# Attention output with four column tiles on TensorE: sums of four key tiles on GpSimd, row maxima transposed before they are negated

## The reference

```python
Q = Q * cos + rotate_half(Q) * sin
K = K * cos + rotate_half(K) * sin
scores = jnp.einsum('bhqd,bhkd->bhqk', Q, K) / scale
scores = jnp.where(causal, scores, -jnp.inf)
attn = jax.nn.softmax(scores, axis=-1)
out = jnp.einsum('bhqk,bhkd->bhqd', attn, V)
return out.transpose(0, 2, 1, 3).reshape(B, S, H) @ Wo.T + bo
```

## Time and profile before

| | before |
|---|---|
| median of 3 runs (lowest to highest) | 755.08 us (752.31 to 756.74) |
| the profiled execution: its time | 756.7 us |
| its span in the profile | 754.9 us |
| TensorE busy, granted clock | 732.0 us, 0.995 of full speed |
| VectorE, ScalarE, GpSimd busy | 442.2, 308.7, 246.4 us |
| DMA | 104.39 MB, 138 GB/s mean |

### The profile page before, as it was taken

The page is one execution under the profiler, slowest core; times in us unless marked ns, Lnnn a source line. Parts: engine busy times, 40 slices in busy tenths (PEclk is TensorE's granted clock), DMA queues, the critical chain, the costliest instruction groups (busy, mean ns, idle before and its releaser), DMA issues.

```text
span 754.9 us, 10665 instructions
## 1 busy us (share of the span) xinstructions
PE 732.0 (97%) x3563; PEld 537.5 (71%) x3563; DVE 442.2 (59%) x1103; ACT 308.7 (41%) x641; POOL 246.4 (33%) x224
## 2 busy tenths in 40 slices
PE   7999999979999999999999999999999999999996
PEld 7788888755665655555555547878788888888884
DVE  6979584987777777777777637863243125114113
ACT  3232232256666666666655562223322232222221
POOL 0626251502114142414141436832232223223222
PEclk9999999999999999999999999999999999999998
DMA  8586568635566666666676475650001001001001
GB/s 281 187 280 232 197 251 278 251 127 158 167 168 180 166 177 181 170 180 175 167 194 167 111 208 171 250 227 1 0 3 55 0 1 56 0 0 56 1 1 58
DMA packets 54318, 104.39 MB, mean 138 GB/s; under 512 B 14820, under 2 KB 18404, under 8 KB 53748
## 3 DMA queue, kind: packets, MB, share of 16 engines
q1 hardware_dynamic: 54264, 103.72, 44.7%
HBM read 69.62 MB, written 38.21 MB: 143 GB/s over the span
## 4 chain that ended last, share of the span: by engine, by line
PE 83%; issue 5%; DVE 4%; DMA 3%; ACT 2%; POOL 2%; SPq 0%; DVEq 0%; POOLq 0%; ACTq 0%
PE ps L1101 38%; PE ps L1240 17%; PE ps L1316 9%; PE ps L1219 8%; PE ps L1126 8%; DMA q_st<-neg_max_T 2%; PE ps L1093 2%; POOL hid_lo L592 1%; ACT p L680 1%; ACT o_raw L687 1%; PE ps L1137 1%; PE ps L1160 1%; SPq L421 0%; DMA x_st<-in_x 0%; DVE stats L796 0%
## 5 line engine op out<-in xcount | busy, mean ns | idle before, releaser
L680 ACT ACTIVATE p<-ps 128x384 f32<-128x384 f32 (+3 forms) x384 | 159.5, 489 | 35.0 <-PE ps L1219 34.4
L841 DVE CUSTOM_DVE_ANT_0 masked<-ps,mask_qk 128x512 bf16<-128x512 f32 (+1 forms) x240 | 113.6, 502 | 66.9 <-PE ps L1126 66.0
L1219 PE MATMUL ps<-q_st,k_st 99*128 99x384 f32 (+2 forms) x384 | 135.6, 361 | 4.2 <-ACT p L680 1.3
L1240 PE MATMUL ps<-p,v_slot 128*64 128x512 f32 (+3 forms) x768 | 137.3, 494 | 0.2 <-ACT o_raw L687 0.2
L1052 DVE SCALAR_TENSOR_TENSOR hid<-ps,us_sb,silu 128x512 f32<-128x512 f32 x44 | 33.0, 751 | 165.2 <-PE ps L1101 159.5
L1126 PE MATMUL ps<-k_st,q_st 96*128 96x512 f32 (+2 forms) x384 | 127.8, 355 | 1.0 <-DVE row_max L841 0.9
L592 POOL TENSOR_TENSOR hid_lo<-hid,hid_hi 128x512 fp32r<-128x512 f32 x44 | 56.8, 1292 | 172.2 <-ACT hid_hi L756 172.2
L561 POOL TENSOR_SCALAR_AFFINE_SELECT p<-p 128x512 f32<-128x512 f32 x64 | 40.7, 637 | 202.9 <-ACT p L680 202.8
L1240 PEld LDWEIGHTS ps<-p,v_slot 128*64 128x64 f32 x768 | 50.1, 136 | 74.3 <-issue 62.0
L1126 PEld LDWEIGHTS ps<-k_st,q_st 96*128 96x128 f32 x384 | 72.5, 190 | 26.4 <-issue 17.7
L1219 PEld LDWEIGHTS ps<-q_st,k_st 99*128 99x128 f32 x384 | 72.3, 190 | 18.7 <-ACT p L680 9.6
(11 more groups left out here) (119 smaller groups left out, 1081.9 us busy)
## 6 DMA issues: line engine op xcount, KB each, us to landing
qk_scratch<-st_hi SPq DMA_DIRECT2D x32, 512.0 KB, 3.8
q_st<-qk_scratch SPq DMA_DIRECT2D x32, 384.0 KB, 3.9
k_st<-qk_scratch SPq DMA_DIRECT2D x32, 384.0 KB, 5.0
flag_st<-in_ffn SPq DMA_DIRECT2D x32, 264.0 KB, 2.8
ffn_copy<-in_ffn SPq DMA_DIRECT2D x32, 264.0 KB, 3.2
qk_scratch<-st_lo SPq DMA_DIRECT2D x16, 512.0 KB, 3.8
o_T<-o_raw SPq DMA_DIRECT2D x32, 128.0 KB, 4.6
rec_l<-rec_rows SPq DMA_DIRECT2D x32, 128.0 KB, 3.3
```

Source lines behind the costliest of these rows:

```text
L680: act.activation(p32[:, at:at + q0 + w - keep], ps[:, ST_BANK + i % ST_RING, keep - q0:w], ACT.Exp, scale=SCALE).then_inc(exp_done, 1)
L841: ins = dve.tensor_tensor_reduce((masked_a if u < 2 else masked)[:, s_before(i) % 2, col:col + kept], scores, mask_qk[:, 512 - kept:512], ...
L1219: pe.matmul(ps[:, ST_BANK + i % ST_RING, 0:w], k_st[0:K_ALL, slot, kt * P:(kt + 1) * P], q_st[0:K_ALL, slot, q0:q0 + w], start=True, stop= ...
L1240: ins = pe.matmul(ps[VW * a:VW * (a + 1), o_bank(u, half), q0 - 512 * half:512], v_slot[:, slot, kt, :], p32[:, at:at + n], start=(kt == 0 ...
```

## The change

P of key tiles 0 to 3 has no mask in the second half of the queries. The changed kernel sums these four tiles there, once for each head, on GpSimd (`sum_p`, three additions of 128x512), between the two masks, and takes l of those keys from one product with the sum. The products of the second half have 32 weight columns, and each head has two column tiles of its own: "v" rows (V of key tiles 0 to 3 or 0 to 5) and, in the other 32 rows, "l" (ones with P or with the sum) and "w" (V of the last two key tiles, in other PSUM columns). The second half is cut in two quarters of 256 queries, parts 1 and 2. "v" and "w" are two parts of the same result, so o_raw gets 512 more columns, SyncE two more moves for a pair (to o_w), and GpSimd one more addition for four heads. The inverses are loaded into the last group of o_T, and for the last group into a buffer in the place of P. The output weights are loaded at head 30 and not at the start. VectorE's test is done in two halves. The maxima are transposed at entry 3, ahead of the group, as they are; ScalarE writes the negated high word out of PSUM, VectorE the low one.

The core of the diff ("..." marks what is left out):

```diff
-M_ENTRY = 4
-M_AFTER = 3
+M_ENTRY = 3
+M_AFTER = 2
 S_BANKS = [[piece] for piece in S_PIECES[:-2]] + [S_PIECES[-2:]]
 S_BANKS.insert(M_ENTRY, [])
...
-PV_GROUPS = [[(0, 0), (0, 1), (0, 2), (0, 3)], [(1, 0), (1, 1)], [(1, 2), (1, 3), (1, 7)], [(1, 4), (1, 5), (1, 6)]]
+PV_GROUPS = [
+    (0, [[("vl", 0)], [("vl", 1)], [("vl", 2)], [("vl", 3)]]),
+    (1, [[("v", 0), ("w", 4)], [("v", 1), ("l", None)], [("v", 2), ("l", 4)], [("v", 3), ("l", 5)], [("w", 5)]]),
+    (2, [[("v", 0), ("w", 6)], [("v", 1), ("l", None)], [("v", 2), ("l", 4)]]),
+    (2, [[("v", 3), ("l", 5)], [("v", 4), ("l", 6)], [("v", 5), ("l", 7)], [("w", 7)]]),
+]
...
+PARTS = 3
+PART_DONE = (2, 4, 4)
+QW = 256
+SUM_KT = KT // 2
+SUM_SLOTS = 3
...
-            o_raw = sb("o_raw", [P, 2, S], F32, under_xT)
-            rec_l = sb("rec_l", [P, S], F32, under_xT)
+            o_raw = sb("o_raw", [P, 2, S + 2 * QW], F32, under_xT)
...
+                sp.wait_ge(o_evac, PARTS * (u + 1))
                 if u % 2 == 0 and u >= 2:
                     sp.wait_ge(l_out, 16 * (u // 2))
+                if u == PAIRS - 2:
...
                     t = 2 * u + a
                     rows = slice(t % 4 * D, (t % 4 + 1) * D)
-                    sp.dma_start(o_T[rows, t // 4, :], o_raw[2 * D * a:2 * D * a + D, u % 2, :]).then_inc(o_moved[u % 2], 16)
-                    sp.dma_start(l_cols[:, t % 4, :], o_raw[2 * D * a + D:2 * D * a + D + 1, u % 2, :].rearrange("o (p e) -> o p e", e=KT)).then_inc(o_moved[u % 2], 16)
+                    v_rows, l_rows = slice(VW * a, VW * a + D), slice(VW * a + D, VW * (a + 1))
+                    sp.dma_start(o_T[rows, t // 4, :], o_raw[v_rows, u % 2, 0:S]).then_inc(o_moved[u % 2], 16)
+                    sp.dma_start(l_cols[:, t % 4, :], o_raw[VW * a + D:VW * a + D + 1, u % 2, 0:S].rearrange("o (p e) -> o p e", e=KT)).then_inc(o_moved[u % 2], 16)
+                    sp.dma_start(o_w[t // 4 % 2][rows, :], o_raw[l_rows, u % 2, S:S + 2 * QW]).then_inc(o_moved[u % 2], 16)
 
             def store_rec(g):
...
                     load_head(t + SLOTS, t % SLOTS)
+                if t == HEADS - 2:
+                    sp.wait_ge(st_ps, NPC * t)
...
 
                 pool.wait_ge(rec_in, 64 * (g + 1))
-                pool.tensor_tensor(o_T[:, g, :], o_T[:, g, :], rec_l[:, :], ALU.mult).then_inc(o_scaled, 1)
+                pool.tensor_tensor(o_T[:, g, S // 2:S], o_T[:, g, S // 2:S], o_w[g % 2][:, :], ALU.add).then_inc(o_joined, 1)
+                pool.wait_ge(o_joined, g + 1)
+                pool.tensor_tensor(o_T[:, g, :], o_T[:, g, :], rec_of(g), ALU.mult).then_inc(o_scaled, 1)
                 pool.wait_ge(o_scaled, g + 1)
                 pool.tensor_scalar(o_T[:, g, :], o_T[:, g, :], bv_sb[:, g % KC:g % KC + 1], None, ALU.add).then_inc(o_done, 1)
...
+            def sum_p(t):
+
+                def second_half(kt):
+                    at = t % SLOTS * P_SIZE + P_OFF[kt] + S // 2 - P * kt
+                    return p32[:, at:at + S // 2]
+
+                total = p_sum[:, t % SUM_SLOTS, :]
+                if t >= SUM_SLOTS:
+                    pool.wait_ge(p_sum_read, 2 * ((t - SUM_SLOTS) // 2 + 1))
+                pool.tensor_tensor(total, second_half(0), second_half(1), ALU.add).then_inc(p_sum_step, 1)
+                pool.wait_ge(p_sum_step, 2 * t + 1)
+                pool.tensor_tensor(total, total, second_half(2), ALU.add).then_inc(p_sum_step, 1)
+                pool.wait_ge(p_sum_step, 2 * t + 2)
+                pool.tensor_tensor(total, total, second_half(3), ALU.add).then_inc(p_summed, 1)
+
...
             for t in range(HEADS):
                 copy_v(t)
                 if t % 4 == 0 and t >= 8:
                     scale_group((t - 8) // 4)
-                mask_p(t)
+                mask_low(t)
+                sum_p(t)
+                mask_high(t)
...
+                def max_high(u):
+                    act.wait_ge(max_T_ps, u + 1)
+                    act.activation(neg_hi_T[:, u % 2, :], ps[0:KT, M_BANK, 0:P], ACT.Copy, scale=-1.0).then_inc(max_hi, 1)
...
-            def evacuate_half(u, half):
...
+                act.wait_ge(pv_part[part], PART_DONE[part] * (u + 1))
...
+                    act.wait_ge(o_moved[u % 2], 96 * (u // 2))
+                src = ps[:, o_bank(u, part), :]
+                if part == 0:
+                    act.copy(o_raw[:, u % 2, 0:S // 2], src).then_inc(o_evac, 1)
+                else:
+                    dst = o_raw[:, u % 2, S // 2:S + 2 * QW].rearrange("p (s q c) -> p s q c", s=2, c=QW)
+                    act.copy(dst[:, :, part - 1, :], src.rearrange("p (s c) -> p s c", c=QW)).then_inc(o_evac, 1)
...
+            def whole_max(u):
+
+                dve.wait_ge(s_max, NS * (u + 1))
+                if u > 0:
+                    dve.wait_ge(max_T_ps, u)
+                dve.tensor_reduce(max8[:, :], row_max[:, u % 2, :, :], AX_X, ALU.max).then_inc(max_ready, 1)
+
+            def max_low(u):
+
+                dve.wait_ge(max_hi, u + 1)
+                dve.scalar_tensor_tensor(out=neg_lo_T[:, u % 2, :], in0=ps[0:KT, M_BANK, 0:P], scalar=-1.0,
+                                         in1=neg_hi_T[:, u % 2, :].bitcast(F32), op0=ALU.mult, op1=ALU.subtract).then_inc(max_T, 1)
...
+                for half in range(2):
+                    if t == 0 and half == 0:
+                        dve.wait_ge(flag_init, 1)
+                    else:
+                        dve.wait_ge(flag_done, 2 * t + half)
+                    cols = slice(half * FFN_PIECE // 2, (half + 1) * FFN_PIECE // 2)
+                    dve.scalar_tensor_tensor(out=flag_bits[:, :], in0=flag_st[:, cols].bitcast(I32), scalar=(1 << 12) - 1,
+                                             in1=flag_bits[:, :], op0=ALU.bitwise_and, op1=ALU.bitwise_or).then_inc(flag_done, 1)
...
             def transpose_max(v):
                 pe.wait_ge(max_ready, v + 1)
-                if v + 1 < HEADS:
-                    pe.wait_ge(s_max, NS * (v + 1) + s_before(M_ENTRY - S_RING) + 1)
                 if v > 0:
                     pe.wait_ge(max_T, v)
-                pe.transpose(ps[0:2 * KT, M_BANK, 0:P], neg_max[:, :].bitcast(F32), ident[:, :]).then_inc(max_T_ps, 1)
+                pe.transpose(ps[0:KT, M_BANK, 0:P], max8[:, :], ident[:, :]).then_inc(max_T_ps, 1)
...
+            def output_product(u, a, part, kind, kt):
+
+                slot, bank = (2 * u + a) % SLOTS, o_bank(u, part)
+                q_end = S // 2 if part == 0 else S // 2 + QW * part
+                q_low = 0 if part == 0 else q_end - QW
+                q0 = q_low if kt is None else max(P * kt, q_low)
+                if kt is None:
+                    probs = p_sum[:, (2 * u + a) % SUM_SLOTS, q0 - S // 2:q_end - S // 2]
+                else:
+                    at = slot * P_SIZE + P_OFF[kt] + q0 - P * kt
+                    probs = p32[:, at:at + q_end - q0]
+                row = VW * a
+                if kind == "vl":
+                    rows, weights, col = slice(row, row + VW), v_slot[:, slot, kt, :], q0 - q_low
+                elif kind == "v":
+                    rows, weights, col = slice(row, row + D), v_slot[:, slot, kt, 0:D], q0 - q_low
+                elif kind == "l":
+                    rows, weights, col = slice(row + D, row + VW), v_slot[:, slot, 0, D:VW], q0 - q_low
+                else:
+                    rows, weights, col = slice(row + D, row + VW), v_slot[:, slot, kt, 0:D], QW + q0 - q_low
+                ins = pe.matmul(ps[rows, bank, col:col + q_end - q0], weights, probs,
+                                start=((kind, part, kt) in PV_FIRST), stop=((kind, part, kt) in PV_LAST), skip_group_check=True)
+                if kt is None and part == 2:
+                    ins.then_inc(p_sum_read, 1)
+                if (kind, part, kt) in PV_LAST and kind != "l":
+                    ins.then_inc(pv_part[part], 1)
+
...
+                part, rounds = PV_GROUPS[group]
...
+                elif group == 1:
+                    pe.wait_ge(p_summed, 2 * u + 2)
                     pe.wait_ge(p_high_masked, 2 * u + 2)
...
+                for products in rounds:
                     for a in range(2):
...
+                        for kind, kt in products:
+                            output_product(u, a, part, kind, kt)
```

More of the change, by code:

```diff
@@ L273, in transformer_block @@
         p_high_masked = sem("p_high_masked")
-        pv_half = [sem(f"pv_half{k}") for k in range(2)]
+        p_sum_step = sem("p_sum_step")
+        p_summed = sem("p_summed")
+        p_sum_read = sem("p_sum_read")
+        pv_part = [sem(f"pv_part{k}") for k in range(PARTS)]
         o_evac = sem("o_evac")
@@ L338, in t_bank, with o_bank, rec_of @@
             return MM_BANK + j if n == N_CH else T_BANK + (j + 2) % TJ
-        def o_bank(u, half):
-            return ST_BANK if (u, half) == (PAIRS - 1, 1) else O_BANK
+        def o_bank(u, part):
+            return (O_BANK, ST_BANK + 2, ST_BANK)[part] if u == PAIRS - 1 else O_BANK
+        def rec_of(g):
```

(2 more changed lines are left out.)

133 lines of the change are left out of this document (56 added, 77 removed).

## The result

The changed kernel takes 761.99 us (median of 4 runs, 758.43 to 763.00), the one before 753.71 beside it. The ratio is 1.0081, 95% interval 1.0046 to 1.0116: **slower by 0.8%**, where a faster kernel, 749 us, was forecast. The profiled execution took 761.53 us, its span is 760.0. That of the kernel before (756.7 and 754.9) lies 3.0 us above its median, so the spans differ by 5.1 us where the medians differ by 8.3.

What follows compares the result with a forecast made beforehand. TensorE, busy 97% of the span, was taken as the bound. Terms -20.5 - 1.0 - 1.5 + 9 + 8.3 = -5.7 us took the span from 754.9 to 749.2; forecast 749 us, range 736 to 768.

Steps and rivals of the forecast that it cites:

- output products, four tiles at once: Stage B, second half: four column tiles overlap fully, 768 columns fewer, -1.28 us a pair, -20.5 us over 16 pairs.
- early transposes and what they free: Maxima transposed ahead of group 0: cost and freed exponential taken as 0; early transposes no longer waiting for the negation, -1.0 us.
- DMA stalls of the maxima: Maxima leave for q_st earlier in odd steps, so TensorE stands less for them: -1.5 us (bounds 0, -2.5).
- six post-scaling steps: VectorE's test meets GpSimd's sums after a scaling; score banks wait about 1.5 us, six times: +9 us (bounds 0, +11.4).
- to the last pair's start, in sum: Forecast terms for stage B up to the last pair's start, together -12.7 us.
- last pair and passage (-1.3 + 8.3): End of stage B into C1: last pair's shorter groups -1.3 us, late chunk 2 +8.3 us.
- I take 0 for the two, bounds -6 and +6: Stage B: transpose waiting 0.1 to 0.2 us a step, against some 0.4 us a pair from the exponential; net 0.
- The collisions: After scalings, test halves on VectorE each wait for the end of a GpSimd addition; TensorE's score banks wait 1.5 us.
- The passage: Stage B to C1: late sums, scalings and moves start chunk 2 5 to 9 us late, +8.3 us (bounds +5, +10).
- the rival of 805: Output products: only two run at a time, groups 1 to 3 3.0 us a pair longer, about 805 us; chance 0.16.
- Masks and copies: By the skill's port rule these GpSimd instructions also delay VectorE's test: 0.4 us in 14 steps, 5 us more, 754.
- GpSimd as the bound: Rival in stage B: additions at 1.75 us make GpSimd the bound and eat the gain, 758 to 768; chance 0.13.

Runs made afterwards that it cites:

- e6: Kernel before the change with 64 unused bytes laid between xT and everything above it: 761.69 us, ratio 1.0076 to before.
- e9: Changed kernel with 192 more unused bytes between xT and everything above it, a multiple of 256 bytes apart again: 755.00 us, ratio 0.9991 to before.
- e5: Changed kernel with 64 more unused bytes between xT and everything above it: 759.83 us, ratio 1.0057 to before.
- e1: Changed kernel with 96 unused bytes a partition laid under xT, moving all later tiles together: 760.88 us, ratio 1.0074 to before.
- e12: e9 with each of VectorE's test halves cut from 264 columns to 8, most weights untested: 747.56 us, ratio 0.9915 to before.
- e8: e5 with GpSimd's sums cut from 512 columns to 8 from the fourth head on: 758.20 us, ratio 1.0024 to before.
- e11: e9 with the maxima transposed after the first group again (M_ENTRY 4, M_AFTER 3, as before the change): 769.82 us, ratio 1.0186 to before.

## Why the prediction was wrong, step by step

| step of the prediction | forecast | measured |
|---|---|---|
| output products, four tiles at once | -1.28 a pair | -1.30 a pair |
| early transposes and what they free | 0, and -1.0 | third gap +0.37 a pair, others +0.04 to +0.13 |
| DMA stalls of the maxima | -1.5 | second gaps -2.0 |
| six post-scaling steps | +9 | +3.6 |
| to the last pair's start, in sum | -12.7 | -10.7 |
| last pair and passage (-1.3 + 8.3) | +7.0 | +10.9 |
| stage A, C2 | no term | +0.8, +4.1 |

Between the -5.7 us of the sum and the +5.1 of the two spans lie 10.8 us: 4.9 in stage A and C2, 3.9 in the last pair and the passage, 2.0 in the pairs before.

- **The step that failed is one that isn't there.** The sum has no term for C2 and stage A, since their instructions are the same. The run of tile sizes in the diff moved xT against the weights by a distance that isn't a multiple of 256 bytes; e6 and e9 show it both ways: 4.8 to 5.0 us in C2's matmuls; in the medians 6.7 us (e6 over the 755.02 beside it) and 4.8 to 5.9 (e5 and e1 over e9). With it repaired (e9) the change makes no difference that can be measured, 0.9991.
- **"I take 0 for the two, bounds -6 and +6"** was mis-sized. Both parts came as told: the transpose costs TensorE 0.16 us in most steps, and the exponential gave 0.3 us back. But that balances only the even steps. In the odd ones nothing was given back, and smaller delays came with the new order: the score bank behind a group takes 0.34 us to the next start, and the piece ahead of a group 0.40 where it took 0.33. +6 us was the upper bound; the lengthened gaps make +5.5 in the third and about +1.7 in the others over 15 pairs. The -1.0 for the early transposes belongs ahead of the first output products and was booked with the pairs; there those waits did go.
- **The collisions** are the right mechanism at 0.6 us, not 1.5: a test half lost half a microsecond, not a whole addition. That error went the other way.
- **The passage** went as told, in its cause, its place and its wait (4.9 us ahead of chunk 2, 0.6 ahead of chunk 1, 2.2 in the last pair, where 1.3 was said; 7.7 us together, 8.3 in the sum). What the forecast left out is the slower mask (0.9 of the 2.2 us) and the clock behind the waits, 4.2 us: -1.3 + 7.7 + 4.2 = 10.6 of the 10.9.
- **Output products**: the Trainium skill (TensorE: Matmul & The Clock Gate, Part 3, "The mechanism") has matmuls start and end in program order. The prediction drew from this that four tiles would be no faster than two, which doesn't follow: tiles that start together and end together keep that order. Groups 2 and 3 take 1.43 and 1.44 us, which only four overlapping tiles give, so the rival of 805 fell. The order of products isn't refuted by it; only the two records of one product don't both come ahead of the next product's first, as rows 4 showed before.
- **Masks and copies**: by the Trainium skill (SBUF — State Buffer, the rules on the shared port pair) they collide with the test as well. The copy's median is 589 ns in the changed kernel, 399 without the test (e12) and 397 without the sums (e8), so the rule holds for the copy; the masks stay at 0.64 us but for two, and the last pair's. But plain gaps are the same in e12, so it cost TensorE nothing, where 5 us stood in the prediction for it.
- **GpSimd as the bound** fell: the additions took 1.28 us in the median and 1.45 at the most.

## What to carry to other kernels

A resized buffer is part of a change: before costing stages "untouched", compute where the moving operands and the weights of their matmuls now lie, and look at the start-to-start time of the same matmul before and after (227 against 233 ns is invisible in busy time). An engine's work that was free inside a loop is paid in full where the loop ends: cost the last iteration by itself, with each wait priced twice, once as idle time and once as the lower clock that can follow it. And a piece moved ahead pays in every step for stalls that it spares in a few: here 0.4 us in each pair, against 3.2 to 6.6 us in six pairs without it (e11).
